# Summing the squared q and k values in two steps, on GpSimd and VectorE, and turning the rotation's crosswise addition into one operation each for q and k

## The reference, cut to what matters

```python
def rotate_half(x):
    x1, x2 = jnp.split(x, 2, -1)
    return jnp.concatenate([-x2, x1], -1)

def attn_layer(x, Wqkv, qs, ksc, Wo):        # 16 heads of 64
    q, k, v = jnp.split(x @ Wqkv, 3, -1)     # then split by head
    q = l2norm(q) * qs                       # t / max(norm of t over the 64, 1e-12)
    k = l2norm(k) * ksc
    q = q * cos * scale + rotate_half(q) * sin * scale
    k = k * cos * inv + rotate_half(k) * sin * inv
    return local_attention(q, k, v) @ Wo     # windows of 32 tokens, softmax

for i in range(6):
    x = attn_layer(shift_tokens(x), ...) + x
    x = ffn_layer(shift_tokens(x), ...) + x
```

## Time and profile before

| | |
|---|---|
| median of 3 executions | 1905.65 us (1899.59 to 1909.58) |
| the profiled execution | 1908.25 us, its span 1906.3 us |
| granted TensorE clock, mean over the span | 0.956 of full speed |
| TensorE busy | 1774.9 us, 93% of the span |
| VectorE busy | 1527.7 us, 80% |
| GpSimd busy | 1260.5 us, 66% |
| ScalarE busy | 1138.3 us, 60% |

### The profile page before, as it was taken

One profiled execution on the slowest core, in us unless ns is written; L12 is line 12 of the kernel. 1 busy time (PEld: TensorE's weight loads), 2 busy tenths in 40 slices (PEclk: granted clock), 3 DMA queues, 4 the chain that ended last, 5 costly groups with the idle time before them and its releaser, 6 DMA issues.

```text
span 1906.3 us, 73037 instructions
## 1 busy us (share of the span) xinstructions
PE 1774.9 (93%) x31224; PEld 1201.0 (63%) x31224; DVE 1527.7 (80%) x2117; ACT 1138.3 (60%) x2221; POOL 1260.5 (66%) x981
## 2 busy tenths in 40 slices
PE   7699976999999989999899999899998999999985
PEld 2255653566666766666676766666766666767663
DVE  6599847888888878888788888688887888888853
ACT  5533224576767656667567676567674767676742
POOL 3477734877777757777577777577776777777730
PEclk9799967999999989999899999899999999999987
DMA  4545002222222232222422223222223322222220
GB/s 97 127 61 75 1 3 81 69 69 66 72 69 72 79 103 69 69 69 74 122 69 69 69 69 117 68 69 72 69 74 107 80 61 77 68 72 69 71 60 27
DMA packets 68259, 137.28 MB, mean 72 GB/s; under 512 B 17953, under 2 KB 23521, under 8 KB 66913
## 3 DMA queue, kind: packets, MB, share of 16 engines
q1 hardware_dynamic: 67936, 132.62, 27.2%
HBM read 29.79 MB, written 2.10 MB: 17 GB/s over the span
## 4 chain that ended last, share of the span: by engine, by line
PE 42%; DVE 16%; POOL 10%; issue 10%; DMA 10%; ACT 4%; SPq 4%; DVEq 0%; POOLq 0%; ACTq 0%
PE bank L1467 9%; PE bank L1450 7%; PE bank L1377 6%; POOL rot L1315 5%; DMA v_shift<-v_tok 5%; DVE rot L1777 5%; PE bank L1425 5%; PE bank L1382 3%; PE bank L1508 3%; PE bank L1484 3%; DVE rnorm L1783 2%; DVE total L1803 2%; POOL probs L1339 2%; DVE probs L1796 2%; PE bank L1390 2%
## 5 line engine op out<-in xcount | busy, mean ns | idle before, releaser
L1777 DVE TENSOR_TENSOR rot<-bank,gains 128x1024 f32<-128x1024 f32 x384 | 461.9, 1204 | 156.1 <-ACT squares L1610 146.4
L1321 POOL TENSOR_TENSOR rot<-rot,rnorm 128x1024 f32<-128x1024 f32 x192 | 361.2, 1903 | 326.3 <-ACT rnorm L1620 326.3
L1315 POOL TENSOR_TENSOR rot<-rot 128x512 f32<-128x512 f32 x384 | 481.0, 1275 | 7.0 <-DVE rot L1777 7.0
L1377 PE MATMUL bank<-wqkv,x 128*128 128x512 f32 x768 | 403.3, 609 | 5.7 <-DVE v_tok L1756 2.9
L1610 ACT ACTIVATE squares<-bank 128x512 f32<-128x512 f32 x384 | 232.8, 606 | 243.2 <-PE bank L1377 242.6
L1651 ACT ACTIVATE o_T<-bank 128x512 f32<-128x512 f32 x192 | 104.2, 598 | 260.6 <-PE bank L1450 260.6
L1339 POOL TENSOR_TENSOR probs<-probs,total 128x1024 f32<-128x1024 f32 x96 | 182.8, 1904 | 115.9 <-DVE total L1805 115.9
L1783 DVE TENSOR_REDUCE rnorm<-squares 128x16 f32<-128x1024 f32 x192 | 232.8, 1212 | 2.8
L1450 PE MATMUL bank<-p_T,v_shift 64*64 64x32 f32 x6144 | 197.9, 225 | 31.9 <-DMA p_T<-p_blocks 31.6
L1450 PEld LDWEIGHTS bank<-p_T,v_shift 64*64 64x64 f32 x6144 | 171.7, 140 | 84.7 <-issue 56.1
L1390 PEld LDWEIGHTS bank<-st_ident,rot 128*128 128x128 f32 x1536 | 181.5, 144 | 61.1 <-issue 54.7
(11 more groups left out here) (198 smaller groups left out, 2867.5 us busy)
## 6 DMA issues: line engine op xcount, KB each, us to landing
p_T<-p_blocks SPq DMA_DIRECT2D x768, 64.0 KB
v_shift<-v_tok SPq DMA_DIRECT2D x96, 384.0 KB, 3.5
v_shift<-v_tok SPq DMA_DIRECT2D x96, 128.0 KB, 3.4
wqkv<-in_wqkv SPq DMA_DIRECT2D x6, 1536.0 KB, 7.8
v_rep_sb<-v_by_step SPq DMA_DIRECT2D x32, 128.0 KB
v_rep<-v_by_step SPq DMA_DIRECT2D x32, 128.0 KB
wo<-in_wo SPq DMA_DIRECT2D x6, 512.0 KB, 8.5
w<-in_w SPq DMA_DIRECT2D x6, 341.0 KB, 8.7
```

Of the source, the lines that this page charges most:

```text
L1315: nc.gpsimd.tensor_tensor(out=out, in0=out, in1=by_head(turned[:, part])[:, :, frm], op=ALU.add).then_inc(rot_added.sem, 1)
L1321: nc.gpsimd.tensor_tensor(out=by_head(qk[u][:, half]), in0=by_head(qk[u][:, half]), in1=rnorm[u][:, AH * i:AH * (i + 1)].unsqueeze(2).to_b ...
L1377: nc.tensor.matmul(QK_BANKS[i][:, :], shifted_tokens(x, n, P), layer_cols(wqkv, n, 3 * INNER, 512 * i, 512), start=True, stop=True).then_i ...
L1777: nc.vector.tensor_tensor(both, src.unsqueeze(1).to_broadcast([P, 2, 8, DH]), pair_of_gains.unsqueeze(2).to_broadcast([P, 2, 8, DH]), ALU. ...
```

## The change

`norms` becomes two steps: GpSimd adds the upper 32 squares of each head to the lower 32, in place (a new function `halve_squares`, 128x512 out of two operands of 128x512, once for q and once for k), and VectorE sums the 32 that are left instead of 64. VectorE's `norms` waits for GpSimd's `halve_squares` where it waited for ScalarE's `square`. `add_turned` does its two crosswise additions in one operation of 128x1024, whose second operand is read with the halves in reversed order. The counts of the semaphore `rot_added` are halved to match. On GpSimd, `halve_squares` is called right ahead of each `add_turned`.

```diff
         def add_turned(n, i):
             part = slice(INNER * i, INNER * (i + 1))
             pool.wait_ge(rotated.sem, rotated.after(n, 2 * (i + 1)))
-            half = DH // 2
-            for f in range(2):
-                to, frm = slice(half * f, half * (f + 1)), slice(half * (1 - f), half * (2 - f))
-                out = by_head(qk[n % 2][:, part])[:, :, to]
-                nc.gpsimd.tensor_tensor(out=out, in0=out, in1=by_head(turned[:, part])[:, :, frm], op=ALU.add).then_inc(rot_added.sem, 1)
+            halves_of = turned[:, part].rearrange("p (h f d) -> p h f d", f=2, d=DH // 2)[:, :, ::-1, :]
+            out = qk[n % 2][:, part].rearrange("p (h f d) -> p h f d", f=2, d=DH // 2)
+            nc.gpsimd.tensor_tensor(out=out, in0=out, in1=halves_of, op=ALU.add).then_inc(rot_added.sem, 1)
+
+        def halve_squares(n, h):
+
+            pool.wait_ge(squared.sem, squared.after(n, 2 * h + 2))
+            sq = by_head(squares[:, INNER * h:INNER * (h + 1)])
+            low, high = sq[:, :, 0:DH // 2], sq[:, :, DH // 2:DH]
+            nc.gpsimd.tensor_tensor(out=low, in0=low, in1=high, op=ALU.add).then_inc(ss_halved.sem, 1)
...
             at(0, table_gains)
             at(1, unit, 0)
             at(1, unit, 1)
+            at(0, halve_squares, 0)
             at(0, add_turned, 0)
             at(2, unit_probs)
+            at(0, halve_squares, 1)
             at(0, add_turned, 1)
...
         def norms(n, h):
-            dve.wait_ge(squared.sem, squared.after(n, 2 * h + 2))
+            dve.wait_ge(ss_halved.sem, ss_halved.after(n, h + 1))
             dve.wait_ge(qk_made.sem, qk_made.after(n - 2))
-            nc.vector.reduce_sum(rnorm[n % 2][:, AH * h:AH * (h + 1)], by_head(squares[:, INNER * h:INNER * (h + 1)]), AX).then_inc(ss_made.sem, 1)
+            nc.vector.reduce_sum(rnorm[n % 2][:, AH * h:AH * (h + 1)], by_head(squares[:, INNER * h:INNER * (h + 1)])[:, :, 0:DH // 2], AX).then_inc(ss_made.sem, 1)
```

More of the change, by code:

```diff
@@ L1146, in build_stream @@
     qk_product, v_product, squared = sig("qk_product", per=4), sig("st_v_product", per=2), sig("squared", per=4)
-    rotated, rot_added, ss_made, above_floor = sig("rotated", per=4), sig("rot_added", per=4), sig("ss_made", per=2), sig("above_floor")
+    rotated, rot_added, ss_halved, ss_made, above_floor = sig("rotated", per=4), sig("rot_added", per=2), sig("ss_halved", per=2), sig("ss_made", per=2), sig("above_floor")
     rnorm_log, rnorm_made, qk_made, v_read = sig("rnorm_log"), sig("rnorm_made"), sig("qk_made", per=2), sig("v_read", per=2)
@@ L1291, in gpsimd @@
     def gpsimd(pool):
-        for s in (gains_made, rot_added, qk_made, halo_made, p_normed):
+        for s in (gains_made, rot_added, ss_halved, qk_made, halo_made, p_normed):
             pool.sem_inc(s.sem, s.credit * s.per)
@@ L1319, in unit @@
             pool.wait_ge(rnorm_made.sem, rnorm_made.after(n))
-            pool.wait_ge(rot_added.sem, rot_added.after(n, 2 * (i + 1)))
+            pool.wait_ge(rot_added.sem, rot_added.after(n, i + 1))
             nc.gpsimd.tensor_tensor(out=by_head(qk[u][:, half]), in0=by_head(qk[u][:, half]),
@@ L1772, in rotate @@
             if i % 2 == 0:
-                dve.wait_ge(rot_added.sem, rot_added.after(n - 1, 2 * (i // 2 + 1)))
+                dve.wait_ge(rot_added.sem, rot_added.after(n - 1, i // 2 + 1))
             cols, src = slice(512 * i, 512 * (i + 1)), by_head(QK_BANKS[i][:, :])
```

## The result

The changed kernel takes 2017.66 us (median of 4 runs, 2016.44 to 2019.50) against 1907.45 for the kernel before (four executions, one more than in the table of the kernel before): 1.0593 times as long, with a 95% interval of 1.0570 to 1.0615. It is slower, as forecast, by 110 us; forecast were 170.

What follows compares the result with a forecast made beforehand. The prediction took TensorE to bound the stream, with VectorE's `gated_full` having no slack. It added 130.6 us of waits and 40 us of clock to 1908.25, giving 2078.9, forecast as 2076 against the median; range 2018 to 2120 us.

Steps and rivals of the forecast that it cites:

- Both new waits of turn A: VectorE's two sums in turn A wait for GpSimd's halving, starting 2.25 and 4.02 us late; about 2 us idle each.
- the shorter one of turn B: VectorE's second sum in turn B waits again for GpSimd's halving, about 1.4 us idle.
- the absence of a fourth: VectorE's first sum in turn B has no idle time, as its halving ends before VectorE comes to it.
- both stops of TensorE: TensorE stops twice per pair: about 1.3 us before `project_v` 1 and 1.5 us before `up_a_tail`.
- The Trainium skill's rule: Elementwise addition belongs on VectorE; if both engines' time lay on the path, a loss of 0.72 us per halving, 138 us.
- what VectorE saves is worth nothing: TensorE bounds the stream, so VectorE's shorter sums, 0.53 us each, four per pair, are worth next to nothing in themselves.
- the clock, 40 us in the sum: After TensorE's second stop a clock fall costs 1.67 us in full; taken in every second pair, 24 times: 40 us.
- 48 x 2.72 = 130.6: In each of 48 pairs the waits make VectorE's `gated_full` 2.72 us late, holding TensorE's `up_a_tail`: 130.6 us.
- Turn B adds nothing to that: Turn B's lateness is absorbed by VectorE's 2.89 us idle time before the next turn A: no added cost.
- the halving arrives in time: Rival: the halving ends before VectorE's sum needs it, so not slower, 1901 to 1906 us; chance 0.09.
- GpSimd becomes the bound: Rival: the joined addition with reversed operand is much slower, 5 us, making 2213 us; chance 0.06.
- the clock never falls: Rival: TensorE's clock stays full and only the waits cost, 2036 us; chance 0.25.

Runs made afterwards that it cites:

- run 1: The change with only the halving, `add_turned` again two operations of 128x512; against the kernel before: 2023.91 us, ratio 1.0605.
- run 2: The change with only the joined addition, VectorE summing all 64 squares and waiting for ScalarE alone; against the kernel before: 1907.49 us, ratio 0.9994.
- run 4: The change with GpSimd reordered: first halving ahead of `unit`, second ahead of the division, tables ahead of the second addition; against the kernel before: 1917.36 us, ratio 1.0046.
- run 5: The change with only the first halving of a turn moved, ahead of `unit`; against the kernel before: 1938.71 us, ratio 1.0163.
- run 8: The change with halvings into an unread tile, sums of half a head not waiting for them, tables ahead of the second halving; against the kernel before: 1903.41 us, ratio 0.9987.
- Run 3: The change with halvings written to an unread tile, VectorE summing half a head and waiting for ScalarE alone; against the kernel before: 1965.61 us, ratio 1.0291.
- run 6: The change with only the second halving moved, to right behind the first; against the kernel before: 1989.63 us, ratio 1.0417.

## Why the prediction was right, and where it was off

**Right: the mechanism and the sign.** Both new waits of turn A, the shorter one of turn B and the absence of a fourth stand in the timeline within 0.2 us of the working; both stops of TensorE are where they were put, 1.41 and 1.36 us (forecast 1.3 and 1.5), and TensorE is busy for 92% of the stream (forecast 91 to 93). Runs 1 and 2 leave only the halving as the cause, runs 4 and 5 show that it is its place in the queue. GpSimd's idle 3 us ahead of `unit` were of no use behind `unit`, but run 5 puts the halving there, and the first wait is gone. The Trainium skill's rule (GPSIMD Engine Reference, section Engine selection) would have elementwise additions on VectorE; run 8 gives GpSimd that work and loses nothing, so here the rows' reading decides, the place in the queue.

**Right: what VectorE saves is worth nothing.** In run 8 it saves 0.53 us per sum, waits for no halving, and the time is that of the kernel before, as near as the interval tells. Part of what it saves goes into a wait of `turn_p` for GpSimd's division (55 us in 41 waits).

**Mis-sized: the clock, 40 us in the sum.** "After the second it is paid in full", and "I take every second pair": not one of the 41 regular pairs had a fall after the second stop. 18 had one after the first, where the prediction had it cost little, and there it costs 0.34 us, 6 us in all. These 6 are already within the 2.61 per pair.

**Mis-sized: the number of pairs that pay.** 48 x 2.72 = 130.6 was forecast for the waits, in pairs of 33.8 to 35.5 us. Most regular pairs take 33.70. Measured are 2.61 in 41 pairs, 107 us; the four in which the next layer's weights are loaded were already waiting for DMAs and paid nothing, nor did the last two. Counted over the whole stream, 105.6 instead of 130.6, this term and the clock's make 65 us, against the 58 by which the forecast was too high; the 2.5 us by which the first `norm_x` is later go the other way, and the rest is the step from the profiled executions to the medians. That the time still touches the range is luck: its lower end was worked out from 2.4 us in each of 48 pairs and no loss of clock, and not from pairs that pay nothing.

**Incomplete: "Turn B adds nothing to that".** True of the change as it stands, since `gated_full` and the tables were late by nearly the same amount (`rotate` 0 starts 0.09 us after the tables end). The working did follow the tables to `rotate` 0, but stopped where that was no later than `gated_full` made it. Run 3 shows that GpSimd's added work costs 56 us by itself when the tables stand last in the queue, through `add_ffn` and `project_o`, a slack that the prediction never looked up. No rival stood for it.

**The rivals.** That the halving arrives in time fell with the 285 us for which VectorE's sums stand idle. That GpSimd becomes the bound by a slow joined addition fell with 2368 ns. That the clock never falls was the nearest, 2036. It does fall, in 18 pairs, but that costs 6 us; the measured time lies below 2036 because fewer pairs paid, and each a little less.

## What to carry to other kernels

What work costs on an engine with idle time can hang on its place in that engine's queue; here the same operations cost 110 us or 8, by their order alone. So ask what ends last ahead of it, and who waits behind it on both engines. A share of 66% busy said nothing here; moving the same operations past one neighbour took back 79 of 110 us, and a fuller reordering 100. When a wait is taken away and only half of the loss goes, look for the second path that the wait had hidden, and take both away in one run.

## What the runs showed of the hardware

Whether TensorE's clock falls after a short stop could not be read from the stop's length. In the changed kernel a stop of 1.28 us at 1086 was followed by 3.4 us at the 1.2 GHz level, while stops of 1.41 and 1.36 us in the pair at 938 left it at 2.4 GHz, as did the second stop of every regular pair that has one; what decides it stays open. What a fall costs depends on what TensorE would have waited for next: 0.34 us per pair in the change, 1.4 in run 6, with the same 3.4 us at the lower level.

On GpSimd, reading one operand with the halves of each head in reversed order costs next to nothing: 128x1024 takes 2368 ns, and the line through 740 for 256 and 1275 for 512 gives 2345. With an operand that repeats one value per head the time is shorter: `unit`, a multiplication of the same size, takes 1.9 us.
